# Spreading a layer norm over the tiles before it in the first stage of a graph attention and mixture-of-experts kernel

## The reference, cut to what matters

```python
x = x + _L0_gnn_ref(_layernorm(x, axis=-1), adj, W_seq, a1, a2, W_out, b_out)

# _layernorm: (x - mean) / sqrt(var + eps), over the 512 columns of a token
# _L0_gnn_ref begins with:
seq = (x @ W_seq).reshape(N, H, DH)            # N = 2048, H = 16, DH = 32
score1 = jnp.einsum('nhd,d->hn', seq, a1)
score2 = jnp.einsum('nhd,d->hn', seq, a2)
```

## Time and profile before

| what | us |
|---|---|
| median of three runs | 2288.91 |
| lowest and highest of them | 2283.89, 2289.49 |
| span of the profiled execution | 2287.1 |
| PE busy in the span | 2066.2 |
| DVE busy | 1556.2 |
| ACT busy | 1078.5 |
| POOL busy | 585.9 |

### The profile page before, as it was taken

The page is one execution under the profiler, slowest core; times in us unless marked ns, Lnnn a source line. Parts: engine busy times, 40 slices in busy tenths (PEclk is TensorE's granted clock), DMA queues, the critical chain, the costliest instruction groups (busy, mean ns, idle before and its releaser), DMA issues. The chain is left out here.

```text
span 2287.1 us, 42237 instructions
## 1 busy us (share of the span) xinstructions
PE 2066.2 (90%) x17716; PEld 1216.1 (53%) x17716; DVE 1556.2 (68%) x2563; ACT 1078.5 (47%) x1059; POOL 585.9 (26%) x447
## 2 busy tenths in 40 slices
PE   6899999999995899989999999999981699999997
PEld 3554444444442444544444444444430698888886
DVE  6689999999984666658778767677357544444441
ACT  4778988988980323213444444444420322222221
POOL 2510000000002012233454555555330222222211
PEclk8989999999997999959999999999995799999999
DMA  6421212212115013333022030010121544444421
GB/s 237 169 78 51 77 48 71 74 50 74 69 36 198 28 46 120 128 90 82 20 53 60 20 88 24 24 33 23 66 84 68 190 100 108 120 120 120 120 61 23
DMA packets 90905, 185.87 MB, mean 81 GB/s; under 512 B 14332, under 2 KB 23548, under 8 KB 86332
## 3 DMA queue, kind: packets, MB, share of 16 engines
q1 hardware_dynamic: 81756, 162.20, 21.6%
q0 software_dynamic: 8960, 20.98, 4.9%
HBM read 138.47 MB, written 40.23 MB: 78 GB/s over the span
## 5 line engine op out<-in xcount | busy, mean ns | idle before, releaser
L1473 DVE TENSOR_REDUCE t_rm<-t_m 128x1 f32<-128x512 f32 (+3 forms) x640 | 373.0, 605 | 154.2 <-PE t_m L1622 96.6
L1407 ACT ACTIVATE t_E<-t_s 128x1024 f32<-128x1024 f32 (+3 forms) x320 | 277.3, 894 | 417.4 <-PE t_s L1639 226.3
L1369 POOL TENSOR_TENSOR t_total<-t_E 128x1024 f32<-128x1024 f32 (+2 forms) x151 | 291.9, 1944 | 225.0 <-PE t_d L1666 219.3
L573 ACT ACTIVATE m_step<-m_ub,gat_bias 128x2048 bf16<-128x2048 f32 x128 | 250.0, 1989 | 11.1 <-DMA m_ub<-scratch_uac 5.7
L715 PE MATMUL m_bd<-m_mask,m_S 128*32 128x512 bf16 x3072 | 230.2, 379 | 11.0 <-DVE m_mask L663 11.0
L715 PE MATMUL m_bd<-gat_adjT,m_S 128*32 128x512 bf16 x2496 | 201.3, 379 | 4.8 <-PE m_dn L715 4.8
L715 PE MATMUL m_bd<-m_mask,m_neg 128*32 128x512 bf16 x2496 | 188.9, 379 | 0.0
L1997 POOL DMA_INDIRECT out<-e_ye,e_token x40 | 81.3, 2033 | 350.2 <-DVE e_ye L2099 345.4
L2163 PE MATMUL e_h<-e_xTh,e_w1h 128*128 128x320 f32 x512 | 159.5, 312 | 3.6 <-PE e_y L2182 2.2
L2163 PE MATMUL e_h<-e_xTl,e_w1h 128*128 128x320 f32 x512 | 158.8, 310 | 0.0
L2163 PE MATMUL e_h<-e_xTh,e_w1l 128*128 128x320 f32 x512 | 158.8, 310 | 0.0
(11 more groups left out here) (359 smaller groups left out, 4167.8 us busy)
## 6 DMA issues: line engine op xcount, KB each, us to landing
a_adj<-in_adj SPq DMA_DIRECT2D x16, 1024.0 KB, 4.9
m_ub<-scratch_uac SPq DMA_DIRECT2D x16, 1024.0 KB, 5.0
e_w1r<-in_L_ffn_w SPq DMA_DIRECT2D x8, 2048.0 KB
e_w2r<-in_L_ffn_w SPq DMA_DIRECT2D x8, 2048.0 KB, 9.0
tq_Q<-scratch_parts SPq DMA_DIRECT2D x36, 256.0 KB, 4.5
gat_scale<-scratch_uac SPq DMA_DIRECT2D x32, 256.0 KB
scratch_parts<-o_hi SPq DMA_DIRECT2D x32, 256.0 KB, 2.2
scratch_parts<-o_lo SPq DMA_DIRECT2D x32, 256.0 KB, 2.7
```

Of the source, the lines that this page charges most:

```text
L573: act.activation(step(n), ub[h % 2][:, :].rearrange("p (t q) -> p t q", t=T), ACT.Relu, bias=bias[:, j, h:h + 1], scale=BIG).then_inc(step ...
L1369: pool.tensor_tensor(total[:, two, off:BANK], E[a % 3][:, two, off:BANK], E[(a + 1) % 3][:, two, off:BANK], ALU.add).then_inc(summed[z], 1)
L1407: act.activation(E[n % 3][:, two, off:BANK], ps_s[:, two, off:BANK], ACT.Exp, scale=SCALE).then_inc(exp_done[z], 1)
L1473: dve.tensor_reduce(rm[:, h, t, ch:ch + 1], ps_m[i % 2][:, 0:w], AX, ALU.max).then_inc(entry_read, 1)
```

## The change

DVE's `normalise(c)` is taken apart into the statistics of one tile, the variances of a group, the inverses of a group and the normalising of one tile. Group 0 is done as before. Of each later group, DVE does a part at the head of each of the four iterations before it, and the last two tiles of the group at the head of the group's own first iteration. ACT takes the square root of the group in iteration 2, 6 and 10, after the store of the strip before. SP issues the second piece of x after adjacency strip 1, and the third and fourth after strips 4 and 8. PE's and POOL's programs are as they were.

```diff
                 load_adj(0)
                 for a, dst in ((a1, arow[0]), (a2, arow[1])):
                     sp.dma_start(dst[:, :], a.partition_broadcast(P)).then_inc(a_in, 16)
+                load_adj(1)
                 load_x(1)
-                load_adj(1)
-                load_x(2)
-                load_x(3)
                 for t in range(2, T):
                     load_adj(t)
+                    if t in (4, 8):
+                        load_x(t // 4 + 1)
...
                     cast(t)
-                    if t < 3:
-                        root(t + 1)
                     if t >= 1:
                         store(t - 1)
+                    if t % 4 == 2 and t // 4 < 3:
+                        root(t // 4 + 1)
                 store(T - 1)
...
+                def coming(t):
+                    n, r = 4 * (t // 4 + 1), t % 4
+                    if r == 0 and t:
+                        normalise(t + 2)
+                        normalise(t + 3)
+                    if n >= T:
+                        return
+                    if r == 0:
+                        stats_of(n)
+                    if r == 1:
+                        stats_of(n + 1)
+                        stats_of(n + 2)
+                    if r == 2:
+                        stats_of(n + 3)
+                        variances(n // 4)
+                    if r == 3:
+                        inverses(n // 4)
+                        normalise(n)
+                        normalise(n + 1)
...
                 for t in range(T):
-                    if t < 3:
-                        normalise(t + 1)
+                    coming(t)
                     dve.wait_ge(adj_cast, t + 1)
```

More of the change, by code:

```diff
@@ L195, in _, with stats_of, variances @@
                 lk = Link(dve, link)
-                def normalise(c):
-                    four = range(4 * c, 4 * c + 4)
+                def stats_of(t):
+                    if t % 4 == 0:
+                        dve.wait_ge(x_in[t // 4], 16)
+                    dve.bn_stats(stats[:, t, :], X[:, t, :]).then_inc(stats_done, 1)
+                def variances(c):
                     cut = slice(4 * c, 4 * c + 4)
-                    dve.wait_ge(x_in[c], 16)
-                    for t in four:
-                        dve.bn_stats(stats[:, t, :], X[:, t, :]).then_inc(stats_done, 1)
                     dve.wait_ge(stats_done, 4 * c + 4)
-                    for t in four:
+                    for t in range(4 * c, 4 * c + 4):
                         last = dve.bn_aggr(mv[:, t, :], stats[:, t, :])
@@ L206, in normalise, with inverses @@
                     dve.tensor_scalar(ve[:, cut], mv[:, cut, 1], LN_EPS, None, ALU.add).then_inc(ve_ready, 1)
+                def inverses(c):
+                    cut = slice(4 * c, 4 * c + 4)
                     dve.wait_ge(sd_ready, c + 1)
                     root_of_inverse(dve, lk, rstd[:, cut], sd[:, cut], ve[:, cut])
-                    for t in four:
-                        dve.tensor_scalar(X[:, t, :], X[:, t, :], mv[:, t, 0:1], rstd[:, t:t + 1],
-                                          ALU.subtract, ALU.mult).then_inc(xn_ready, 1)
+                def normalise(t):
+                    dve.tensor_scalar(X[:, t, :], X[:, t, :], mv[:, t, 0:1], rstd[:, t:t + 1],
+                                      ALU.subtract, ALU.mult).then_inc(xn_ready, 1)
+                def coming(t):
[17 more added lines that the diff above has]
+                        normalise(n + 1)
                 def dots(t):
@@ L216, in dots @@
                         dve.tensor_reduce(s[:, t, :], prod[n][:, :, :], AX, ALU.add).then_inc(dots_done, 1)
-                normalise(0)
+                for t in range(4):
+                    stats_of(t)
+                variances(0)
+                inverses(0)
+                for t in range(4):
+                    normalise(t)
                 for t in range(T):
-                    if t < 3:
-                        normalise(t + 1)
+                    coming(t)
                     dve.wait_ge(adj_cast, t + 1)
```

## The result

The changed kernel takes 2299.43 us (median of 6 runs, 2294.6 to 2301.25) against 2287.09 us for the kernel before in the same comparison (6 runs, 2283.89 to 2289.49): ratio 1.0054, interval 1.0042 to 1.0066. It is 12.3 us slower. The forecast was 2306, range 2294 to 2312, slower.

What follows compares the result with a forecast made beforehand. PE, busy for 90% of the span, was taken to bound the kernel. Two rounds of 9.3 us plus 1.2 in iteration 12 make 19.8, less 2.2 gained early: +17.6, median 2306, range 2294 to 2312.

Steps and rivals of the forecast that it cites:

- wait for tiles 4, 8, 12, each: Iterations 3, 7, 11: PE idles before the transposes because DVE normalises the tile only now, held by POOL; 5.0 us each.
- the clock's cost behind each: After each wait for tiles 4, 8, 12: PE's clock falls to half, slowing the work behind; 2.46 us each.
- turn in iterations 4, 8, 12 late: Two L210 alternate with POOL's pair, so L224 ends late and PE's turn starts late; 1.2 us each.
- turn in iterations 2, 6, 10 late: L201 and the variances meet POOL's pair, L206 waits, so PE's turn starts late; 0.6 us each.
- turn in iterations 1, 5, 9 late: Two L201 come before L223 and L224, which still ends in time for PE's turn; 0 us.
- gain up to the end of product 3: Start of the first stage: the third product ends at 46.1 instead of 48.3, a gain of 2.2 us.
- stage in all: First stage: all stalls, 19.8 us, less the early gain of 2.2, make it 17.6 us longer.
- Rival 1: At DVE beside POOL's pair: small operations aren't held, only L224 is; +7.2 us, 2296; chance 0.15.
- Rival 2: PE's clock doesn't fall in the 5 us stalls, four falls fewer; +7.8 us, 2297; chance 0.10.
- L310 got in ahead of POOL's pair: Inverses in iterations 3, 7, 11: L280 goes before POOL, L281 and L282 wait instead; transposes move by under 0.1 us.
- The early part: Before tile 4: x lands at 19.7, turn 0 starts at 21.3 instead of 24.43, clock falls as before; gain 2.2 us.
- rival 3: First stage: DVE's chain fits beside POOL and the clock stays up, so not slower; -2.6 us, 2286; chance 0.07.

## Why the prediction was right, step by step

| step of the prediction | forecast, us | measured, us |
|---|---|---|
| wait for tiles 4, 8, 12, each | 5.0 | 4.33 (65.09 less 59.86 + 0.90) |
| the clock's cost behind each | 2.46 | 2.16, 2.28, 2.35 (6.20, 6.32, 6.39 less 4.04) |
| turn in iterations 4, 8, 12 late | 1.2 | 0.90 (49.74 less 49.00 - 0.16) |
| turn in iterations 2, 6, 10 late | 0.6 | 0.56 (59.86 less 59.46 - 0.16) |
| turn in iterations 1, 5, 9 late | 0 | 0 |
| gain up to the end of product 3 | 2.2 | 4.09 (48.32 less 44.23) |
| stage in all | +17.6 | +13.07 |

The measured terms add up: 2 x (0.90 + 0.56 + 4.33) + 2.28 + 2.35 + 0.90 - 4.09 = 13.0. The wait in the table is the lateness of the transposes; the rows show 0.16 less as idle time.

*The whole time* alone would not have settled it. It rose by 12.3 us, halfway between the forecast's 17.6 and what rivals 1 and 2 would give (7.2 and 7.8). The timeline decides between them. And 1.8 of the 6.6 us between 2306 and 2299.43 come only from the forecast's base, 2288.91, the median of three runs of the kernel before; over six it is 2287.09.

*The mechanism* was the one forecast: PE waits for a tile that DVE normalises only now, behind two small operations that each wait for an instruction of POOL, and the clock falls meanwhile. The experiments show three shares of it. Without POOL 2.55 us of the wait stay, POOL adds 1.6, and the clock adds 2.2 behind the wait. The shares are not independent: moving the chain and the first tile one iteration ahead took away the order's share, POOL's and the clock's together.

*The wait was 0.7 too large* in the forecast, for two reasons. L310 got in ahead of POOL's pair. The prediction had this case and said that it would move T by under 0.1. That was wrong: with L310 done, POOL's second instruction holds L312 and not L311, so only L313 follows it and not L312 and L313, and POOL's own pair ends at c+4.50, not 4.59. T stood at c+5.37, not 5.69. The other 0.35 was counted twice: where the turn before is late, PE asks for T only at c+1.04 (59.86 + 0.90 less 59.72), not at c+0.70, and the late turn had its own term already.

*L254 in iterations 4, 8, 12* ended 0.3 earlier than forecast, for POOL's instructions took 1.13 and not 1.27 us once DVE had let them in (46.60 to 47.73 and 48.01 to 49.14).

*The early part* was mis-sized by 1.9, the largest error. x landed at 19.40 and not 19.7, and DVE had L254 of tile 0 done at 20.94. The clock's fall around turn 0 cost 6.62 - 4.94 = 1.7, not 2.46. So c of iteration 3 is 32.66, not 33.9, T follows it 0.3 sooner, and the fall behind T cost 0.3 less.

*What follows the stage* was taken as unchanged. By the profiles it is 3.3 us shorter (the span grew by 9.8, the stage by 13.07). Over the kernels tried here the span less the last turn ranges from 2175.3 (one experiment's 2276.1 - 100.82) to 2184.1 (2284.7 - 100.61), with identical instructions. I have not shown why. The runs of one kernel spread as widely (2283.89 to 2289.49 before), so the 3.3 us may be chance and say nothing of the change. This is also why the whole times of the experiments on loads and on the clock can't be told apart.

*Rivals.* Rival 1 (small operations aren't held) is refuted by L311 and L312. Rival 2 (the clock stays up) by the windows. Of rival 3 the stalls were never under 1.35 us; its price for the order alone, 2.75, is what the short products gave: 2.71, counted like the 4.33 in the table (34.52 less 30.91 + 0.90).

*The rule of the Trainium skill* that was set against the forecast (TensorE: Matmul & The Clock Gate, section Part 1: The HAM clock gate) did not save the clock here: PE's idle of 4.17 us brought a fall each time, 1.7 to 2.0 us after its last matmul. The other one (SBUF — State Buffer, section Who interferes with whom) would, if it held for L253, have added two times 0.6. L253 wasn't held: from 48.54 it took 0.13 us in the middle of POOL's second instruction (47.69 to 49.14), so by this trace a 128x1 operation is not one that waits. (The range allowed 1.9 us for it, where the estimate in the text gives 1.2; neither occurred.)

## What to carry to other kernels

Before work is spread into a loop's idle time, write down for each piece when the next engine asks for its result, in that engine's order. A piece that is late by one iteration costs the whole chain of its iteration, each time round. DVE's idle time beside a busy POOL is not free time: small operations in a dependent chain may each wait for a whole instruction of POOL, so keep them away from its bursts, or give them an iteration of slack. Leave transfers that are needed late behind those needed soon; with two early ones PE waited 2.1 us for a strip's turn, where it waits 0.4 us without them.

## What the runs showed of the hardware beyond what was expected

- A fall of the clock is not fixed by the length of an idle stretch. With POOL's products short PE was idle for 2.55 us three times in the same surroundings; the product behind took 3.60 us once and about 5.3 us twice (5.29 and 5.30). Gaps of 2.95, 1.92, 1.85 and 2.66 us ahead of turn 0 brought none in four of the experiments, 3.25 us did in the changed kernel. With the parts behind L254, PE's waits of 1.27 and 1.28 us for tiles 4 and 8 came with a fall (each stood behind a turn that had itself waited, 1.20 and 0.97 us), and 1.76 us for tile 12 came without one. A stall thus costs 0 or some 1.7 to 2.4 us more than its length, and three equal stalls in one execution can differ in this.
- The fall can come when PE is already at work again. In the changed kernel the granted clock was still 1.00 while PE waited for turn 0 and fell only after it had begun, near 21.9; behind the 1.28 us wait for tile 8 just named it was 1.00 from 54 to 55 and fell near 55.6, with the product begun at 55.52. The transposes then run at full speed (0.66 us) and only the product is slow (5.29).
- Whether DVE waits for POOL depends on the kind of its operation and not on how little it has to do. TENSOR_TENSOR and TENSOR_SCALAR operations of 0.16 and 0.17 us on four values a partition took 1.12 and 1.19. BATCH_NORM_STATS2 kept its time (0.68 us from 47.93, in the midst of POOL's second instruction), and so did L253, a TENSOR_SCALAR on one value a partition.
- POOL waits for DVE as well. In iteration 4 its two instructions took 1.44 and 1.45 us, against 1.27 and 1.26 in iteration 7, each time lengthened by an L215 of DVE that ended 0.3 us into it (46.60 and 48.01).
